# Gated cross-attention and feed-forward on one core: idle transposes around the first transposes, a later request for the key weights, and a new order at the end of the prologue

## The reference, cut to what matters

```python
x = x + tanh(g_xattn) * cross_attention(layernorm(x), ctx)   # 16 x 128 tokens of 256, 16 heads of 64
x = x + tanh(g_ffn)   * quantised_ffn(layernorm(x))          # 256 -> 768 -> 256

def cross_attention(x, ctx):           # ctx: 16 x 128 tokens of 512
    q = heads(x @ Wq) / 8
    k, v = heads(ctx @ Wkv)            # 512 -> 2 x 1024
    k, v = [null_k; k], [null_v; v]    # one extra key and value for all heads
    return layernorm(softmax(q k^T) v @ Wout) * ln_scale + ln_bias
```

## Time and profile before

| what | value |
|---|---|
| time, median of 3 runs | 560.23 us (559.73 to 560.52) |
| the profiled execution | 562.19 us |
| its span, first to last instruction | 560.0 us |
| mean granted TensorE clock in it | 0.979 |
| PE, PEld, DVE, ACT, POOL busy | 92%, 81%, 73%, 56%, 25% |
| HBM read, written | 21.27 MB, 4.19 MB |

### The profile page before, as it was taken

How to read it: one execution, slowest core, us unless ns; L and a number is a source line. 1 busy time by engine, 2 the same in 40 slices (tenths; PEclk the granted TensorE clock), 3 DMA queues, 4 the chain that set the end, 5 groups by cost and what they waited for, 6 DMA issues and landing times. The chain is left out here.

```text
span 560.0 us, 10769 instructions
## 1 busy us (share of the span) xinstructions
PE 513.0 (92%) x3936; PEld 455.6 (81%) x3936; DVE 407.1 (73%) x916; ACT 312.0 (56%) x961; POOL 140.6 (25%) x149
## 2 busy tenths in 40 slices
PE   2989999999999999999999999999789999608897
PEld 2968989988998998899899899887667878505797
DVE  5747877566656665765666676878676979999896
ACT  4744443644364254355435426455378569988992
POOL 1300511231121132123113113134123029920000
PEclk9989999999999999999999999999999999957999
DMA  8932000200110110020011001005001000100033
GB/s 309 310 134 77 1 1 28 69 2 1 56 37 0 56 37 0 0 80 14 0 56 37 0 1 39 1 3 169 1 19 39 0 1 0 39 0 1 1 114 112
DMA packets 18493, 25.85 MB, mean 46 GB/s; under 512 B 1232, under 2 KB 15824, under 8 KB 18464
## 3 DMA queue, kind: packets, MB, share of 16 engines
q1 hardware_dynamic: 18208, 25.17, 13.3%
q0 software_dynamic: 256, 0.30, 0.5%
HBM read 21.27 MB, written 4.19 MB: 45 GB/s over the span
## 5 line engine op out<-in xcount | busy, mean ns | idle before, releaser
L1672 POOL TENSOR_TENSOR probs<-probs,rinv 128x512 f32<-128x512 f32 x64 | 66.5, 1045 | 211.6 <-DVE rinv L1234 211.6
L886 ACT ACTIVATE probs<-bank,nmax 128x128 f32<-128x128 f32 x256 | 91.0, 381 | 25.0 <-DVE nmax L1226 25.0
L631 PE MATMUL bank<-wv,ctxT 128*128 128x512 f32 x384 | 95.0, 404 | 2.5 <-ACT qk L860 2.5
L631 PEld LDWEIGHTS bank<-wv,ctxT 128*128 128x128 f32 x384 | 72.2, 191 | 21.1 <-ACT qk L860 2.7
L623 PE MATMUL bank<-ctxT,wk 128*128 128x256 f32 x672 | 88.9, 282 | 0.0
L623 PEld LDWEIGHTS bank<-ctxT,wk 128*128 128x128 f32 x672 | 83.6, 188 | 0.0
L856 ACT ACTIVATE qk<-bank 128x256 f32<-128x256 f32 (+1 forms) x60 | 24.1, 402 | 95.2 <-PE bank L623 92.8
L1238 DVE COPY pT<-bank 128x512 f32<-128x512 f32 x64 | 41.1, 684 | 42.3 <-PE bank L690 42.1
L886 ACT ACTIVATION_READ_ACCUMULATOR probs<-bank,nmax 128x1 f32 x256 | 56.7, 221 | 0.0
L623 PE MATMUL bank<-xnT,wq 128*128 128x256 f32 x336 | 51.8, 290 | 0.1
L663 PE MATMUL bank<-wout,oT 128*128 128x256 f32 x384 | 47.3, 282 | 1.7 <-DVE oT L1243 0.9
(11 more groups left out here) (167 smaller groups left out, 917.2 us busy)
## 6 DMA issues: line engine op xcount, KB each, us to landing
craw<-in_ctx SPq DMA_DIRECT2D x8, 512.0 KB, 3.8
stage<-in_L_xattn_Wkv SPq DMA_DIRECT2D x8, 512.0 KB, 10.4
xa<-in_x SPq DMA_DIRECT2D x8, 256.0 KB, 2.7
xr<-in_x SPq DMA_DIRECT2D x8, 256.0 KB, 2.8
x_scratch<-y SPq DMA_DIRECT2D x7, 256.0 KB, 2.2
x2all<-x_scratch SPq DMA_DIRECT2D x1, 1536.0 KB, 6.9
xres<-x_scratch SPq DMA_DIRECT2D x6, 256.0 KB, 2.8
out<-yout SPq DMA_DIRECT2D x6, 256.0 KB, 2.2
```

What stands on the lines that cost most here:

```text
L631: last = mm(bk[:, :], ctxT[a][:, k, b * S:(b + 1) * S], wv[w][:, k, h * 512:(h + 1) * 512], start=(k == 0 and i == 0), stop=(k == KC - 1 a ...
L886: nc.scalar.activation(probs[:, p % 2, h, u, :], score_bank[p % 2][h][:, u * S:(u + 1) * S], ACT.Exp, bias=nmax[:, p % 2, h, u:u + 1], acc ...
L1672: G.tensor_tensor(probs[:, p % 2, h, :, :], probs[:, p % 2, h, :, :], rinv[:, p % 2, h, :].rearrange("p (u o) -> p u o", o=1).to_broadcast ...
```

## The change

TensorE: 16 transposes of the identity into a spare bank ahead of the first X, 24 behind it, with results that nothing reads. SyncE: ahead of the first key piece it waits until the first query piece has landed. ScalarE: k6 and the second X are emptied first, then tanh and both halves of the exponentials. VectorE: `constants` moves behind the second X's remainder, `weight_scales(0)` from behind V10 to behind V00.

```diff
@@ sync engine
             for i, (_, src, _, fold) in enumerate(pieces):
                 if i >= NST:
                     sp.wait_ge(wsplit_lo, i - NST + 1)
+                if i == READY_Q:
+                    sp.wait_ge(stage_in[0], 16)
                 sp.dma_start(stage_view(i, fold), src).then_inc(stage_in[i % NST], 16)
@@ tensor engine
+            def idle_transposes(count):
+
+                for _ in range(count):
+                    nc.tensor.transpose(bank[3][:, 0:P], ident[:, :], ident[:, :])
+
+            pe.wait_ge(ident_ready, 1)
+            idle_transposes(16)
             for pos in range(len(PRO)):
                 unit("pro", pos)
+                if pos == 0:
+                    idle_transposes(24)
                 if PRO[pos] == "k4":
                     scores(0, 0)
@@ scalar engine
             while npos[0] < len(PRO):
-                if PRO[npos[0]] == "k6":
+                split("pro", npos[0])
+                if PRO[npos[0]] == "X":
                     act.wait_ge(const_in, 16 * 5)
                     nc.scalar.activation(gates[:, :], gates[:, :], ACT.Tanh).then_inc(tanh_done, 1)
                     exps(0, 0, 0)
-                split("pro", npos[0])
-                if PRO[npos[0]] == "X":
                     exps(0, 0, 1)
@@ vector engine
                 if PRO[npos[0]] == "k6":
                     for h in range(2):
                         maxima(0, 0, h)
+                split("pro", npos[0])
+                if PRO[npos[0]] == "X":
                     constants()
-                split("pro", npos[0])
                 if PRO[npos[0]] == "V00":
                     for h in range(2):
                         inverse_sums(0, 0, h)
+                    weight_scales(0)
                 if PRO[npos[0]] == "V01":
                     dve.wait_ge(ctx_half_hi, 1)
                     low(ctxT[1][:, :, 0:S], craw[:, :, 0:S], ctxT[0][:, :, 0:S])
-                if PRO[npos[0]] == "V10":
-                    weight_scales(0)
```

## The result

The changed kernel takes 558.24 us (median of 7 executions, 556.98 to 559.11) where the kernel before, beside it on the same chip, takes 560.52. The ratio over all executions is 0.9942 [0.9921, 0.9964], so it is faster: 3.25 us less, 557.0 us on the scale of the 560.23 that the prediction starts from. (The medians alone lie 2.28 us apart; the executions of before reach up to 564.04, and the means are 561.40 and 558.03.) The forecast was 554.7 us in a range of 553.6 to 557.8. The direction and the range held; the size, 5.5 us, was too large.

What follows compares the result with a forecast made beforehand. TensorE was taken to bound the kernel, so prologue savings reach the end whole: 3.7 (k6's emptying) + 1.6 (clock) + 0.2 (`weight_scales(0)`) = 5.5 us, from the median 560.23 to 554.7 us, range 553.6 to 557.8.

Steps and rivals of the forecast that it cites:

- k6 ahead of the exponentials: Prologue, ScalarE: k6's bank emptied behind the second output piece's copy, so V00 starts at 31.34, 3.68 us sooner.
- That transfer I leave where it was: First output piece, copied at 28.11, fixes ScalarE's emptying; its transfer was assumed unmoved, as no part of the change touches it.
- sign for a late train: First output piece copied after 29 us would show the forecast wrong, pointing to rival 2 or rival 5.
- rival 2: Prologue transfers 1 to 2 us late as SyncE asks later: V00 at 32.3 to 33.4, 555.7 to 556.8 us; chance 0.12.
- rival 3: Clock gain at V00 not in the timed runs, or the clock still falls in the shorter gap: 556.3 us; chance 0.09.
- The clock at V00: TensorE's gap before V00 shrinks from 2.46 to under 1 us, avoiding half speed: 1.6 us, zero at the low end.
- V11's emptying: VectorE before the first group: moving `weight_scales(0)` frees this emptying, giving TensorE between nothing and 0.3 us, taken as 0.2.
- The transposes: TensorE around the first X: q0 at full speed from 10.5, k0 resumes at 18.1, helping k6 end early; no separate gain.
- Rival 1: Transposes do not lift the clock at q0: V00 0.4 us earlier to 0.6 us later, 558.0 to 559.0 us; chance 0.11.
- The hold: SyncE's wait before key pieces: second query piece lands between 6.25 and 8.29, taken as 7.3; called doubtful; no separate gain.
- Rivals 4 and 5: Gain taken up later by another engine in the groups, about 560 us, chance 0.04; or hold makes it slower, chance 0.05.
- rival 5: Hold starves the transfers, so ScalarE empties k4 and k6 late: gain gone from 5.5 us late, 562.7 at 8; chance 0.05.

Runs made afterwards that it cites:

- e9: Kernel before plus the 40 idle transposes and SyncE's wait alone, without the new order on ScalarE and VectorE: 562.82 us, ratio 1.0021.
- e6: Changed kernel with k2 and k4 emptied a place sooner, both output pieces copied and subtracted behind the exponentials, block scales back behind V10: 557.84 us, ratio 0.9930.
- e4: Changed kernel with the gain and bias loads asked for by SyncE behind the feed-forward weights and `constants` behind V11: 557.10 us, ratio 0.9929.
- e1: Changed kernel without SyncE's wait ahead of the key pieces: 558.07 us, ratio 0.9947 to the kernel before.
- e3: Changed kernel without SyncE's wait and without the idle transposes, only the new order on ScalarE and VectorE left: 558.40 us, ratio 0.9949.
- e5: Changed kernel with ScalarE emptying k2 ahead of the fourth value piece's copy and k4 one place sooner: 558.37 us, ratio 0.9960.
- e11: Same as e10 but without the 40 idle transposes: 558.46 us, ratio 0.9947 to the kernel before.
- e8: Same as e6 but without the 40 idle transposes: 558.70 us, ratio 0.9953 to the kernel before.
- e10: Changed kernel without SyncE's wait, gain and bias loads behind the feed-forward weights, k2 and k4 emptied one place sooner: 557.37 us, ratio 0.9941.
- e12: Same as e10 but with the idle transposes in loops of eight: 556.57 us, ratio 0.9927 to the kernel before.

## Why the prediction was right, and where it was too high

**k6 ahead of the exponentials, 3.7 us counted, 1.83 found.** The failed step is "That transfer I leave where it was", said of the first output piece as the point that fixes ScalarE's work. It gave the reason that no part of the change touches the transfers. But in the changed kernel the first output piece is copied at 29.25 without a wait, and what held ScalarE was the fourth value piece ahead of it, whose place at 24.63 came from one profile. In eight other profiles, all that have GpSimd's two loads where they were, e9 with the old order among them, the fourth value piece was copied at 25.65 to 27.61, not 24.63. A second thing was missing from the text: k2's emptying stands behind that copy in ScalarE's order, so a late piece delays k6's products and not only the output pieces. e6 takes that emptying and the output pieces out of the way, and with the piece as late V00 comes 1.19 us sooner; e4 takes the loads out of the way, and V00 comes at 31.25. Whether 24.63 was a lucky landing of the kernel before is open: it was not profiled again. The prediction's own sign for a late train, the first output piece copied after 29, is there (29.25), and V00 at 33.19 lies in its rival 2 (32.3 to 33.4), 555.7 to 556.8 us. That the measured 557.0 falls in the range is due to the range, which took in rivals 2 and 3, and not to the sum. The cause that this rival gave, SyncE asking later because of the hold, is not the one: e1 and e3 have no hold and a late piece too.

**The clock at V00, 1.6 us counted.** In the profiles it is there to the tenth, 1.57 us. From 35 to 39 us the changed kernel has:

```profile
35.00:39.00 4.00, 4.00 (x19) 3.25 (x18) 3.47 (x9) 2.02 (x14) 1.67 (x2) 1.00 0.03 10
```

19 products, where the earlier trace rows has 10 at a clock of 0.57. But the doubt that the prediction kept as its low end and as rival 3 was justified. Every timed execution lists a mean clock beside its span. Of the 63 of before, 24 had 0.979, the profiled one's, with spans of 559.3 to 561.8 and a mean of 560.3; 26 had 0.982, that of the changed kernel's profile, with 557.2 to 558.9 and a mean of 558.1. Of the other 13, two at 0.978 had 557.7 and 558.1, and eleven at 0.973 or 0.976 had 558.9 to 561.5. So 35 of the 63 were about 2 us longer, and the mean of 559.2 lies 1.1 us, and not 1.6, over that of the executions at 0.982. That those 35 lost their time at V00 was seen only in the profiled one, and a lower mean clock is no proof of it: e5's profiled execution, at 0.978, and e11's, at 0.975, have more falls behind the door (a clock of 0.76 and 0.78 from 395 to 402 us, 0.83 from 515 to 525 in e11) and still take 510.8 and 510.9 us from there to the end. Among executions at 0.982 the changed kernel's mean span is 555.3, 2.8 under before; over all executions it is 3.9. Of the 3.9, 1.1 for the clock and 0.15 for V11 leave 2.6 us for k6 in a typical execution (an estimate), between the 3.7 counted and the 1.83 of the profiles.

**V11's emptying, 0.2 counted:** 0.15 found, from `weight_scales(0)` in its new place: from the V units' end to the first group it is 1.02 us here, and 1.17 in e9, which has the old one, as before. V01's bank made no wait.

**The transposes, "worth nothing beyond making the first term whole".** That was wrong on average. The first 16 cost nothing, as said (they end at 5.27, ahead of X). The 24 took 4.39 us and not 3.0, as the clock rose only among them, but they held q0 by no more than 0.1 us: it started at 11.47 and not at 10.5 because the second query piece was copied at 8.42 and not at 7.3, and 8.42 + 2.97 is 11.39. With the 48 products in 5.93 us, k0 resumed at 18.90, 1.34 us sooner than before (18.1 was forecast). In the changed kernel k6 then waited for ScalarE, which hides such sooner work; in the pair with this order (e1 and e3) the transposes were worth 0.5 us of span, and 1.3 in the two pairs where k2 is emptied ahead of the late piece and k6's own end sets V00 (e6 and e8, e10 and e11). Rival 1 falls: 48 products in 5.93 us are 0.124 us each, full speed by the earlier trace rows. The rule that stood beside it, in the Trainium skill, page "TensorE: Matmul & The Clock Gate", section "Part 4: PE-mode transpose", that full speed does not engage for transposes, is not what these float32 transposes show: the 48 products behind them took 5.93 to 6.04 us in all nine kernels that have them, and 7.32 to 8.41 in the five that have none. X behind the first 16 took 0.63 us in e4 and e12 and 1.08 or 1.09 in the other seven, so those 16 lifted the clock in two of the nine only.

**The hold,** called doubtful, brings nothing: the second query piece was copied between 7.04 and 8.92 in the kernels with it, and between 7.26 and 8.36 in those without. The rule of the Trainium skill, page "DMA: Bandwidth & Descriptors", section "Queues, rings and completion order", that each DMA engine takes descriptors in ring order, agrees: key requests made behind the query's were not in its way.

**Rivals 4 and 5.** Neither came. What is won at the first group's door, 3.55 us, is in the span whole (3.6), as in the other profiles. What rival 5 feared, a slower kernel, needs the new order to be absent (e9).

**A term that was missing:** 0.6 us outside the span (2.73 on average against 2.13). With it the means agree: 3.9 us less span and 0.6 more around it are 3.3, beside the 3.25 of the ratio.

## What to carry to other kernels

Before an engine is made faster, find the instruction that stands in a fixed order ahead of the release that counts. Here only a new order moved the release: the order alone brought 0.9949, a faster start alone 1.0021. A landing time read from one profile under a busy DMA is an estimate with microseconds on both sides, so ask what else in the consumer's order stands behind that landing. Work that only warms an engine is worth trying in a loop, and its worth should be judged on many spans rather than on one profile. And a fall of the clock has to be priced where it stands: the one at V00 cost 1.57 us in the profiles, those behind the door in e5 and e11 nothing.

## What the runs showed that was not expected

**Time outside the span grew with straight idle transposes.** With forty more instructions on TensorE, 24 of 66 executions spent 2.37 to 3.70 us outside the span; all six of e12's, with loops, spent 2.14 to 2.24. In the packed trace, the profiled executions of the changed kernel, e1, e4, e5 and e10 have an instruction read of 16 KB that begins behind the last instruction of the span (at 558.2 us of the changed kernel's, whose span ends at 556.4). Those five spent 2.57 to 3.21 us outside. The other nine have none there (before's last such read is at 545.9) and spent 2.06 to 2.19. That this read costs the time is likely, and argued only.

**Two 128 KB loads** slow the DMA engines from 342 to 221 GB/s over 5.5 us at the same busy share. In the changed kernel's trace their 64 packets of 4096 bytes take 0.16 to 1.74 us each, half of them over 0.5.

**A faster start can cost clock later.** In e9 TensorE reached its gap sooner, the gap grew from 2.46 to 3.21 us, and the V units took 14.12 us where they had taken 12.98, in one profile of each; the mean spans, 560.5 and 559.1 on the same chip, point the same way.
